# Slot attention in a two-layer decoder: each pass written out as one order of steps, prefix sums copied by ScalarE and inverted in four parts

## The reference

```
q, k = rope(h @ Wq.T), rope(h @ Wk.T);  v = h @ Wv.T;  g = h @ Wg.T
s  = exp(clip((h @ Ws1.T) @ Ws2.T + bs2, -32, 32))      # token x slot
z  = cumsum(s, axis=token)                              # prefix sums
ok = causal(q @ k.T * DK**-0.5) @ s / z                 # token x slot
p  = softmax(ok, axis=slot)
o  = causal((p / z) @ s.T) @ v
o  = rmsnorm(o) * g_norm_weight * silu(g)
x  = x + o @ Wo.T
```

## Time and profile before

| | |
|---|---|
| median of 3 runs | 1915.8 us (1906.06 to 1917.16) |
| the profiled execution | 1916.61 us, of which the span in the trace 1914.7 us |
| PE, DVE, ACT, POOL busy | 1700.4, 1268.8, 856.7, 560.2 us |
| granted clock of TensorE, mean | 0.947 |

### The profile page before, as it was taken

One profiled execution on the slowest core, in us unless ns is written; L12 is line 12 of the kernel. 1 busy time (PEld: TensorE's weight loads), 2 busy tenths in 40 slices (PEclk: granted clock), 3 DMA queues, 4 the chain that ended last, 5 costly groups with the idle time before them and its releaser, 6 DMA issues.

```text
span 1914.7 us, 51411 instructions
## 1 busy us (share of the span) xinstructions
PE 1700.4 (89%) x21686; PEld 1186.2 (62%) x21686; DVE 1268.8 (66%) x2850; ACT 856.7 (45%) x1404; POOL 560.2 (29%) x951
## 2 busy tenths in 40 slices
PE   5999999999977888899899989997888889899988
PEld 4888888888855346555466545664554445566557
DVE  7766667675656877778888553444356687789844
ACT  3333333433333164556656722441232465567652
POOL 5544434433314140230501022441111222322230
PEclk9999999999988799999999989998897999999999
DMA  3000000110004636334263374655602134554100
GB/s 114 31 12 12 23 34 2 34 57 12 17 3 97 115 57 147 59 93 97 45 143 68 67 264 149 216 179 119 127 1 48 36 74 92 115 110 80 33 2 23
DMA packets 91857, 143.94 MB, mean 75 GB/s; under 512 B 14870, under 2 KB 60123, under 8 KB 91628
## 3 DMA queue, kind: packets, MB, share of 16 engines
q1 hardware_dynamic: 87228, 127.79, 28.6%
q10 hardware_dynamic: 2528, 7.74, 1.2%
q0 software_dynamic: 1872, 5.13, 0.7%
HBM read 109.68 MB, written 32.03 MB: 74 GB/s over the span
## 4 chain that ended last, share of the span: by engine, by line
PE 64%; DVE 20%; ACT 6%; issue 6%; POOL 2%; DMA 1%; SPq 1%; DVEq 0%; another core or an unknown queue 0%; ACTq 0%; POOLq 0%
PE bank L1045 17%; PE bank L1253 6%; PE bank L1998 5%; DVE shared L1326 3%; PE bank L1884 3%; PE bank L777 3%; PE bank L1886 3%; PE bank L1885 3%; PE bank L2017 3%; DVE xa_part_max L1326 3%; PE bank L2460 2%; PE bank L2445 2%; ACT xa_e L1287 2%; PE bank L742 2%; DVE da_neg L2579 1%
## 5 line engine op out<-in xcount | busy, mean ns | idle before, releaser
L1326 DVE TENSOR_REDUCE xa_part_max<-bank 128x1 f32<-128x448 f32 (+1 forms) x512 | 266.2, 567 | 23.5 <-PE bank L1045 21.3
L1287 ACT ACTIVATE xa_e<-bank 128x1024 f32<-128x1024 f32 (+1 forms) x208 | 212.2, 1024 | 131.3 <-PE bank L1045 129.6
L1287 ACT ACTIVATE ca_e<-bank 128x1024 f32<-128x1024 f32 (+2 forms) x208 | 197.2, 958 | 81.8 <-PE bank L1045 79.6
L1326 DVE TENSOR_REDUCE shared<-bank 128x1 f32<-128x400 f32 (+1 forms) x384 | 205.6, 569 | 33.9 <-PE bank L1045 30.2
L1045 PE MATMUL bank<-xa_kst,xa_qst 122*32 122x448 bf16 (+1 forms) x2048 | 183.9, 354 | 16.0 <-DVE xa_part_max L1326 8.1
L1253 PE MATMUL bank<-xa_e,xa_vaug 128*17 128x256 f32 (+1 forms) x1664 | 135.4, 383 | 7.6 <-issue 3.5
L1045 PE MATMUL bank<-xa_qst,xa_kst 128*32 128x256 bf16 (+1 forms) x3264 | 136.5, 276 | 5.1 <-issue 3.2
L1253 PE MATMUL bank<-ca_e,ca_vaug 128*17 128x256 f32 (+2 forms) x1664 | 128.8, 377 | 10.0 <-issue 6.2
L981 POOL TENSOR_TENSOR gsa_qk<-gsa_qk,gsa_rot 128x512 f32<-128x512 f32 x64 | 81.9, 1279 | 164.7 <-DVE gsa_rot L897 164.7
L1045 PE MATMUL bank<-xa_wkv,shared 128*32 128x256 f32 (+1 forms) x1632 | 114.3, 393 | 9.7 <-SPq L281 3.2
L1045 PEld LDWEIGHTS bank<-xa_qst,xa_kst 128*32 128x32 bf16 (+1 forms) x3264 | 94.0, 97 | 36.3 <-issue 8.1
(11 more groups left out here) (408 smaller groups left out, 4232.9 us busy)
## 6 DMA issues: line engine op xcount, KB each, us to landing
xa_kst<-xa_k_parts SPq DMA_DIRECT2D x96, 200.1 KB, 5.0
ca_kst<-ca_k_parts SPq DMA_DIRECT2D x96, 200.1 KB, 5.1
xa_k_parts<-xa_parts SPq DMA_DIRECT2D x24, 400.2 KB, 4.3
ca_k_parts<-moe_ctx_parts SPq DMA_DIRECT2D x8, 1200.8 KB
moe_gu<-in_expert_gate_up SPq DMA_DIRECT2D x8, 1024.0 KB
shared<-in_ctxT_split ACTq DMA_DIRECT2D x4, 1601.0 KB, 9.7
moe_ctxT<-in_ctxT SPq DMA_DIRECT2D x8, 800.5 KB, 8.1
ca_cv<-in_ctx SPq DMA_DIRECT2D x4, 1536.0 KB
```

The lines of the kernel that those rows point to most:

```text
L1287: e.activation(self.e[m % 3][0:rows, :, first:T], banks[m % 2][0:rows].rearrange("p a (h t) -> p (a h) t", t=T)[:, :, first:T], ACT.Exp, s ...
L1326: e.tensor_reduce(top, work[:, 0:hi - lo], AX.X, ALU.max).then_inc(*reduced(t, *step))
```

## The change

For passes m = 0 to 14 the woven order is replaced by a table, `turn(m)`, which gives the steps of a pass one after the other; the passes 15 to 18 are woven as before. Two operations change in all units. The prefix sums `cs` leave the ring of DVE's two banks and go to ACT's ring of three, and ACT copies them into `enz`. The inversion becomes a step of its own, `inverse`, of four DVE reciprocals of 128x128 in place in `enz`, placed among the next pass's rotations.

```
+            def turn(m):
+                g, r = divmod(m, B)
+                s, p = G4 * m, 2 * (m - 2)
...
+                for step in (
+                    ("qk", s), ("a", s - 2), ("inverse", m - 1, 0), ("sm_exp", m - 2), ("scale", m - 3, 0), ("a", s - 1),
+                    ("u", m), ("ok", s - G4), ("rr", m - 3), ("ok", s - 3), ("inverse", m - 1, 1), ("gate", p),
+                    ("v", m - 1, 0), ("qk", s + 1), ("ok", s - 2), ("z", p), ("gate", p + 1), ("scale", m - 3, 1),
+                    ("z", p + 1), ("w2", p, 0), ("qk", s + 2), ("a", s), ("w2", p, 1), ("v", m - 1, 1),
+                    ("es", m), ("ot", m - 3, 0), ("qk", s + 3), ("ok", s - 1), ("inverse", m - 1, 2), ("o", p),
+                    ("w2", p + 1, 0), ("inverse", m - 1, 3), ("w2", p + 1, 1), ("wo", m - 3, 0), *parts[0], ("cs", m),
+                    ("a", s + 1), ("sm_max", m - 1), ("ot", m - 3, 1), ("o", p + 1), ("wo", m - 3, 1), ("et", m),
+                    *parts[1]):
...
+                    if 0 <= m - 1 < GSA_UNITS:
+                        yield "inverse", m - 1, s % G4
...
-                main = list(weave(list(weave(list(scores(m)), list(ahead(m)))), list(behind(m)), lead=8))
+                if m < GSA_UNITS - 1:
+                    main = list(turn(m))
+                else:
+                    main = list(weave(list(weave(list(scores(m)), list(ahead(m)))), list(behind(m)), lead=8))
...
-            "es": [(on_dve, clipped)], "cs": [(on_dve, enz_ready)], "qk": [(on_dve, rotated)],
+            "es": [(on_dve, clipped)], "qk": [(on_dve, rotated)],
+            "cs": [(on_act, cs_copied)], "u": [(on_act, u_ready)], "et": [(on_act, et_ready)], "v": [(on_act, v_ready)], "a": [(on_act, a_copied)],
...
+                elif kind == "cs":
+                    if n >= 3:
+                        q.wait_ge(sm_ready, n - 3)
+                    q.wait_ge(cs_mm, n)
+                    e.copy(enz[n % 3][:].rearrange("p i n -> p (i n)"), home(kind, j)).then_inc(*cs_copied(*step))
...
-                    e.reciprocal(enz[n % 3][:].rearrange("p i n -> p (i n)"), home(kind, j)).then_inc(*enz_ready(*step))
+                elif kind == "inverse":
+                    k, = rest
+                    some = enz[n % 3][:, k // 2, k % 2 * P:(k % 2 + 1) * P]
+                    q.wait_ge(cs_copied, "cs", n)
+                    e.reciprocal(some, some).then_inc(*enz_ready(n, k))
...
-                    q.wait_ge(enz_ready, "cs", n)
+                    q.wait_ge(enz_ready, n, G4 - 1)
```

More of the change, by code:

```diff
@@ L456, in build @@
         es_ready, enz_ready, et_mm, et_ready = (local("gsa", n) for n in ("es", "enz", "et_mm", "et"))
+        cs_copied = local("gsa", "cs_copied")
         v_mm, v_ready = local("gsa", "v_mm"), local("gsa", "v")
@@ L555, in project @@
                     yield from list(norm_steps(1, n % B))[:-TB]
+            def turn(m):
+                g, r = divmod(m, B)
+                s, p = G4 * m, 2 * (m - 2)
+                parts = [[], []]
+                for part, at_, key in ((0, 2, "q"), (1, 2, "k"), (0, 3, "v")):
+                    if r == at_ and g + 1 < GROUPS:
+                        parts[part].append(("w_split", g + 1, key))
+                if r == 0 and g < GROUPS:
+                    if g == 0:
+                        parts[0].append(("w_split", 0, "v"))
+                    parts[0].append(("w_split", g, "g"))
+                if r == 1 and g < GROUPS:
+                    parts[0].append(("wo_scale", g))
+                if r == 3 and g and g + 1 < GROUPS:
+                    parts[1].append(("wo_load", g + 1))
+                units = {"qk": G4, "ok": G4, "a": G4, "z": 2, "w2": 2, "gate": 2, "o": 2}
+                for step in (
[7 more added lines that the diff above has]
+                    *parts[1]):
+                    kind, n = step[:2]
+                    if kind in ("w_split", "wo_scale", "wo_load") or 0 <= n // units.get(kind, 1) < (B if kind == "u" else GSA_UNITS):
+                        yield step
             def xa_early(m):
@@ L607, in build @@
         gsa_order = placed(gsa_steps(), {
-            "es": [(on_dve, clipped)], "cs": [(on_dve, enz_ready)], "qk": [(on_dve, rotated)],
-            "u": [(on_act, u_ready)], "et": [(on_act, et_ready)], "v": [(on_act, v_ready)], "a": [(on_act, a_copied)],
+            "es": [(on_dve, clipped)], "qk": [(on_dve, rotated)],
+            "cs": [(on_act, cs_copied)], "u": [(on_act, u_ready)], "et": [(on_act, et_ready)], "v": [(on_act, v_ready)], "a": [(on_act, a_copied)],
             "z": [(on_act, z_ready)], "w2": [(on_act, w2_copied)], "ot": [(on_act, ot_ready)],
@@ L616, in home @@
         def home(kind, j):
-            return bank[(0 if kind in ("es", "cs", "qk") else 6 if kind in ("gate", "o", "wo", "norm_turn") else 3) + j]
+            return bank[(0 if kind in ("es", "qk") else 6 if kind in ("gate", "o", "wo", "norm_turn") else 3) + j]
         def ok_bank(n):
@@ L880, in gsa_dve @@
                     e.tensor_scalar(es[n % 2][:].rearrange("p i n -> p (i n)"), home(kind, j), CLAMP, -CLAMP, ALU.min, ALU.max).then_inc(*clipped(*step))
-                elif kind == "cs":
-                    if n >= 3:
-                        q.wait_ge(sm_ready, n - 3)
-                    q.wait_ge(cs_mm, n)
-                    e.reciprocal(enz[n % 3][:].rearrange("p i n -> p (i n)"), home(kind, j)).then_inc(*enz_ready(*step))
+                elif kind == "inverse":
[3 more added lines that the diff above has]
+                    e.reciprocal(some, some).then_inc(*enz_ready(n, k))
                 elif kind == "qk":
```

## The result

The changed kernel takes 1862.7 us (median of 4 runs, 1860.85 to 1869.96), the kernel before, beside it on the same chip, 1914.8 us (4 runs, 1906.06 to 1917.16). That is 52 us between the medians; the ratio is 0.9737, with a 95% interval of 0.9698 to 0.9776, so 2.6% less. The forecast was 1877 with a range of 1868 to 1902.

What follows compares the result with a forecast made beforehand. PE was taken as the bound, losing time to waits and slow clock. Passes 4 to 14 give 37.0 us, the first passes 4.3, less 3 for hand-overs: 38.3 less, 1878 profiled, 1877 by median; range 1868 to 1902.

Steps and rivals of the forecast that it cites:

- the floor of a pass: Passes 4 to 14: PE needs 29.8 us a pass in any order, so 327.8 in place of 364.8, 37.0 less.
- The later parts: Passes 15 to 18 keep their order, could move 1 us either way; nothing counted from there on.
- The second way: A check of the floor in passes 4 to 14: (364.8 - 24.3 - 14.6) / 11 = 29.6 us a pass.
- A wait of 0.2 us in each of 15 passes is 3.: Allowance for hand-overs between engines, about 0.1 us each without a row; 3 us taken off the gain.
- The first passes: Passes 0 to 3: of 7.7 us idle, three waits of together 3.4 stay, so 4.3 us less.
- the walk: The new order followed with PE never waiting, each step's start in a 29.8 us pass checked against DVE, ACT and POOL.
- the 441.6 named for that case: Start of pass 15 in us if PE has no wait: 482.87 - 41.3.
- a tight place: `z` to `w2`: ACT's copies end at 9.95 us of a pass, `w2` is due at 10.8, 0.85 to spare.
- The rival of one wait in each pass: One wait, 0.8 us in the middle, with half a slow stretch in 15 passes: 22 us, so 1896; chance 0.17.
- A quarter reads 0.95 us: Each 128x128 reciprocal on DVE in SBUF takes 0.95 us, also beside POOL; four take 3.8.
- the rival on the other side: The quarters collide with POOL, 1.65 us more each: passes of 34.8 us, 25 us slower than before, 1941; chance 0.07.
- The other half of the prediction's reading: A DVE instruction with two SBUF inputs contends with a POOL instruction reading SBUF; L909 took 2.34 us, otherwise 0.69.

Runs made afterwards that it cites:

- near_w2: The changed kernel with the first `w2` of a pass put directly behind its `z`; 1888.1 us in one execution.
- near_cs: The changed kernel with the prefix sums `cs` put directly behind the column sums `es`; 1898.4 us in one execution.
- control_after: The changed kernel, unchanged, timed again in a later set with a second trace; median 1871.0 us, ratio 0.9744 to the kernel before.
- table_bank: The changed kernel, table kept, but `cs` back in DVE's ring and inverted by one 128x512 reciprocal from its bank; 1869.5 us, ratio 0.9733 to the kernel before.
- table_to_17: The changed kernel with the table also for passes 15 to 17, the next block's norm steps behind it; 1865.7 us, ratio 0.9719 to the kernel before.
- bank_to_17: `table_bank` with the table also for passes 15 to 17, the next block's norm steps behind it; 1863.3 us, ratio 0.9763 to the kernel before.
- woven_quarters: The changed kernel without its table: all passes woven, ACT's copy and the four reciprocals kept; 1906.7 us, ratio 0.9911 to the kernel before.
- near_cs_long: `near_cs` with one more 128x512 clip on DVE into a spare tile ahead of the real one; 1910.9 us.

## Why the prediction was off

The mechanism was right: the table takes PE's waits away, and they were what passes 4 to 14 could lose. Four terms of the sum were sized wrongly; the largest in the profiled pair comes first, and the largest that repeats, the floor of a pass, second.

**The later parts were counted at nothing, and had no width.** From the start of pass 15 to the end, the two traces differ by 9.6 us. Of these 1.4 lie in the block's last passes (132.3 to 130.9), and 8.2 behind the block, where nothing was changed. There the granted clock of PE differs by itself: the changed kernel gave 1291.3 and 1298.9 us, the kernel before 1299.5 and 1302.8, each program in two executions, and the time at 1.2 GHz accounts for nearly all of it, as shown above. At the end of the block the lead is 47.6 and 48.3 us, and the medians' lead is 52.1 and 47.7, so most of this term is chance between executions. Against the 47.7 the forecast of 38.3 falls short by 9.4, which is what the three terms below and the 1.4 make: 6.1 + 3 - 1.2 + 1.4 = 9.3. It is also what the range lacked: the runs of the kernel before spread over 11 us, and the low end of 1868 stands only 9 below the forecast, a distance that the next two terms use up by themselves.

**"I take 29.8 us as a pass's floor on PE."** It is 29.25, which is 6.1 us in 11 passes. The stretch of the earlier trace rows from which it was taken begins right behind a wait of 0.45 us, holds one of 0.31 and ends where the next wait begins. The listed idle time was left out, but a wait costs 0.2 to 0.3 us beyond its listing, as `near_w2` and `near_cs` show, and that stayed in as PE's busy time: once for the wait inside and once for the two at the edges, some 0.5 us. The second way, 364.8 less idle time and less clock, has the same fault: it left out what the 24 waits of the earlier trace rows cost beyond their listing, and 14.6 us for the clock came from a rounded 0.96, where eight stretches of 3.4 us at half clock lose 13.6. The 43.1 us gained are 24.3 idle, 13.6 of clock and 5.2 beyond the listing, 0.22 a wait.

**"A wait of 0.2 us in each of 15 passes is 3."** No wait is listed in passes 4 to 14. A hand-over does take some time (0.14 us in `near_w2`), but it runs within the distance that the order gives, and the 3 us had no row behind them.

**The first passes** gained 3.1 us, not 4.3. The two larger of the three waits that the walk left are there, `ok` for its mask with 1.7 us (forecast 1.9) and `qk` 3 for a rotation with 1.0 (forecast 1.2); a slow stretch at 44.9 us, right behind the `ok` wait, granted clock 0.98 in that window, took back 1.7.

Summed: 9.6 + 6.1 + 3 - 1.2, less 0.2 around the span, is 17.3 us, the difference between the 55.6 of the profiled executions and the 38.3 forecast.

What held:

- Pass 15 begins at 436.7 us, with no wait in the 11 passes before it; the 441.6 named for that case erred by the floor.
- The walk found a tight place and nearly its size: 0.85 us at `w2` with the hand-over taken off; the copies end 0.71 us ahead of `w2`, 0.57 with the hand-over of 0.14. The rival of one wait in each pass did not come about, and `near_w2` shows its price where it does: the last sum into x begins at 586.8 us there and at 566.4 in `control_after`, 20.4 us, near the 22 that the rival named. That the two are so near is luck: here 13 passes wait 1.25 us and lose 0.31 more without any slow stretch in them, where the rival had 15 waits of 0.8 us and half a slow stretch behind each.
- A quarter reads 0.95 us, as taken from 8 and 512 columns, and it does not meet POOL. Of the 64, none is longer than 954 ns, given in this order as shortest, median, longest:

```profile
L925 DVE RECIPROCAL gsa_enz<-gsa_enz x64: 894/950/954, 41.4 to 491.2; 128x128 f32<-128x128 f32 x64
```

and 61 of them ran beside POOL, 22 of which began while a POOL instruction was already at work. Two examples, one ahead of POOL's add for the rotation, one begun within a weight split:

```profile
194.32 0.95 DVE L925 RECIPROCAL gsa_enz<-gsa_enz 128x128 f32<-128x128 f32 x1
206.68 0.95 DVE L925 RECIPROCAL gsa_enz<-gsa_enz 128x128 f32<-128x128 f32 x1
```

```profile
194.37 1.27 POOL L1021 TENSOR_TENSOR gsa_qk<-gsa_qk,gsa_rot 128x512 f32<-128x512 f32 x1 [3.43 <-DVE gsa_rot L937]
...
204.65 2.36 POOL L1013 TENSOR_TENSOR gsa_wk<-gsa_w,gsa_wk 128x1024 fp32r<-128x1024 f32 x1 [4.53 <-ACT gsa_wk L838]
```

So the rival on the other side falls, and with it what the Trainium skill ("SBUF — State Buffer", Who interferes with whom) says of an instruction with one SBUF input agrees with this trace for a reciprocal too. The other half of the prediction's reading, that two inputs in SBUF do meet POOL, is seen too: L972 of `rr`, which reads `gsa_ss` and `gsa_rt`, takes 0.17 us alone and 1.23 us beside POOL's product for `sm_exp`, until that ends.

```profile
179.07 1.29 POOL L1027 TENSOR_TENSOR gsa_sm<-gsa_sm,gsa_enz 128x512 f32<-128x512 f32 x1
179.15 1.23 DVE L972 SCALAR_TENSOR_TENSOR gsa_rv<-gsa_ss,gsa_rt 128x8 f32<-128x8 f32 x1
```

The walk left this wait of 1.06 us out. It comes in 10 of the 12 passes of the table that have an `rr`, and PE's list of waits stays empty with it.

- ACT's copy of `cs` cost nothing: 0.585 us a pass, on an engine that is busy 140 of 322 us.

One point stays open. The five leads of medians of kernels whose passes take 29.25 us are 52.1 (the change), 47.7 (again), 53.5 (`table_bank`), 53.0 (`table_to_17`) and 47.0 (`bank_to_17`), 50.7 on average. By the traces the block ends 47.6, 48.3, 53.2, 50.4 and 47.5 us earlier, 49.4 on average. So the gain is made in the block, and nothing that can be told from chance is added behind it. But the last passes of the block, woven in each kernel that follows, took 126.7 us in `table_bank` and 130.9 and 130.7 in the changed kernel, at granted clocks of 0.96 and 0.93, and 129.5 in `woven_quarters`, whose last passes are those of the changed kernel; one execution of each doesn't say whether the copy and the quarters cost that much in the woven passes.

## What to carry to other kernels

Where one engine is busy for nine tenths of a span, as PE is here, walk the order of its queue and ask of each step how far ahead its input was issued on the other engines; an order in which each distance is longer than its chain needs no faster helper, and cutting a long operation into parts then brought nothing here. Take the floor of such a loop from spacings of instructions in a full stream, never from busy time around a wait. And give what lies behind the change a width of its own, as wide as two executions of one program differ there.

## What the runs showed of the hardware

- A wait of TensorE costs 0.20 to 0.31 us more than the idle time listed for it: 0.31 in `near_w2`, 0.27 in `near_cs`, 0.20 in `near_cs_long` and 0.22 over the 24 waits of the kernel before. The last two are what is left when 1.7 us is taken for each slow stretch. The view's matmul spans overlap in a full stream, and the overlap ends at a wait.
- Waits of 1.93 to 1.96 us in passes 4 to 14 of the kernel before were followed by 3.4 us at 1.2 GHz in 13 of 14 cases (two executions); waits of 2.23 us in 6 of 11; the 22 waits of 1.25 and 1.64 us in `near_w2` and `near_cs` in none, nor were four of 1.66 us in `woven_quarters`, but 1.6 and 0.4 us close together in the kernel before were. In passes 0 to 3 waits of 1.72 and 1.73 us were in 4 of 5 traces, one of 1.57 was, and one of 1.90 was in one trace of the kernel before and not in the other. So a longer wait makes a slow stretch likelier at one place, but no length was found that decides it. The Trainium skill ("TensorE: Matmul & The Clock Gate", What's actually happening) says that what sets the clock watches TensorE's recent activity on a beat that runs freely and does not start anew with the kernel. That the same wait is followed by a slow stretch in one pass or execution and not in another agrees with it; no run here moves a wait against that beat alone. A slow stretch of 3.4 us costs 1.7, as two traces of the kernel before with eight and with seven of them show (364.8 and 363.1 us), almost as much as the wait ahead of it.
- VectorE's reciprocal takes 6.25 ns a column of 128 rows and some 0.15 us besides: 0.95 us for 128 columns in SBUF, 3.35 for 512 there and 3.36 from PSUM. Cut in four it costs 0.44 us more. Of 64 reciprocals of 128x128 in SBUF, 61 beside GpSimd instructions, none took over 0.954 us, while a VectorE instruction with two SBUF inputs waited for GpSimd's to end (0.17 us became 1.23).
